# The edges' fields behind the second block's low parts and its first encoder group, and two statistics moved ahead of the edges' copy

## The reference, cut to what matters

```
h  = relu(layernorm(x))                       # x is 1250 x 1024
e  = sigmoid(h @ wenc.T + benc)               # 1250 x 500
h2 = e @ conv_weight                          # 1250 x 500
agg = segment_sum(h2[src] * edge_weight, dst) # 20000 edges, sorted by dst
x  = x + (agg + e @ lin_weight.T) @ wdec.T + bdec
h  = relu(layernorm(x))
x  = x + D^-1/2 (A + I) D^-1/2 (h @ W.T + b)  # A: the same edges
```

## Time and profile before

| | |
|---|---|
| median of 3 runs | 470.28 us (470.02 to 470.74) |
| the profiled execution's own time | 471.0 us |
| its span, first to last instruction | 469.1 us |
| PE busy | 461.9 us, 98% |
| DVE busy | 317.0 us, 68% |
| ACT busy | 208.0 us, 44% |
| granted TensorE clock | 0.999 of full speed (2.4 GHz) |

### The profile page before, as it was taken

One profiled execution on the slowest core, in us unless ns is written; L12 is line 12 of the kernel. 1 busy time (PEld: TensorE's weight loads), 2 busy tenths in 40 slices (PEclk: granted clock), 3 DMA queues, 4 the chain that ended last, 5 costly groups with the idle time before them and its releaser, 6 DMA issues.

```text
span 469.1 us, 9224 instructions
## 1 busy us (share of the span) xinstructions
PE 461.9 (98%) x3452; PEld 401.6 (86%) x3452; DVE 317.0 (68%) x594; ACT 208.0 (44%) x412; POOL 47.0 (10%) x62
## 2 busy tenths in 40 slices
PE   7999999999999999999999999999999999999997
PEld 6999999978888888889888878888889988888886
DVE  6999997777857851594668886928552467567642
ACT  6986797645541141232444444547442522222220
POOL 3722110000000000000000000465500000000000
PEclk9999999999999999999999999999999999999999
DMA  8720848482214570639530005161969415546542
GB/s 306 261 82 23 156 83 219 126 316 77 70 64 85 114 245 0 114 110 342 201 120 1 0 1 213 58 247 68 369 235 381 139 44 226 203 179 224 198 167 99
DMA packets 46111, 72.35 MB, mean 154 GB/s; under 512 B 25292, under 2 KB 34142, under 8 KB 44402
## 3 DMA queue, kind: packets, MB, share of 16 engines
q1 hardware_dynamic: 45746, 71.34, 46.1%
q0 software_dynamic: 320, 0.39, 0.4%
HBM read 44.33 MB, written 22.01 MB: 141 GB/s over the span
## 4 chain that ended last, share of the span: by engine, by line
PE 78%; DVE 9%; DMA 5%; ACT 4%; issue 2%; POOL 2%; POOLq 0%; DVEq 0%; SPq 0%; ACTq 0%
PE bank L1429 18%; PE bank L1445 18%; PE bank L1430 18%; PE bank L1431 18%; DVE weighted L1349 3%; DMA row_scratch<-dis 2%; PE bank L1547 2%; DMA raw<-adj_scratch 2%; DMA dis_row<-row_scratch 1%; PE bank L1549 1%; PE bank L1551 1%; DVE stats L1062 1%; ACT before L874 1%; PE bank L1567 1%; DVE deg L1301 1%
## 5 line engine op out<-in xcount | busy, mean ns | idle before, releaser
L1445 PE MATMUL bank<-a,h_hi 128*128 128x256 f16 (+3 forms) x400 | 85.5, 270 | 0.0
L1445 PE MATMUL bank<-a,h_lo 128*128 128x256 f16 (+3 forms) x400 | 85.5, 270 | 0.0
L1429 PE MATMUL bank<-right,left 128*128 128x512 f32 (+1 forms) x148 | 56.1, 379 | 0.0
L1430 PE MATMUL bank<-right,left 128*128 128x512 f32 (+1 forms) x148 | 55.9, 378 | 0.0
L1431 PE MATMUL bank<-right,left 128*128 128x512 f32 (+1 forms) x148 | 55.9, 378 | 0.0
L1414 DVE SCALAR_TENSOR_TENSOR x<-bank,dis_u,x 128x512 f32<-128x512 f32 (+2 forms) x37 | 26.7, 721 | 36.0 <-PE bank L1431 35.8
L1026 ACT CAST left<-zs 128x512 fp32r<-128x512 f32 x35 | 21.6, 624 | 61.2 <-PE bank L1431 61.1
L1429 PE MATMUL bank<-unit,g 128*128 128x500 f32 (+3 forms) x120 | 42.3, 353 | 0.4 <-DVE unit L1286 0.4
L1445 PEld LDWEIGHTS bank<-a,h_hi 128*128 128x128 f16 (+1 forms) x400 | 39.0, 97 | 4.1 <-issue 0.3
L1445 PEld LDWEIGHTS bank<-a,h_lo 128*128 128x128 f16 (+1 forms) x400 | 39.1, 98 | 3.7
L1431 PE MATMUL bank<-unit,g 128*128 128x500 f32 (+3 forms) x120 | 42.3, 352 | 0.0
(11 more groups left out here) (163 smaller groups left out, 1110.2 us busy)
## 6 DMA issues: line engine op xcount, KB each, us to landing
right_scratch<-right SPq DMA_DIRECT2D x5, 2048.0 KB, 8.2
right<-right_scratch SPq DMA_DIRECT2D x5, 2048.0 KB, 8.0
whole<-w SPq DMA_DIRECT2D x7, 1024.0 KB, 7.5
adj_scratch<-stage SPq DMA_DIRECT2D x50, 125.0 KB, 2.1
raw<-adj_scratch SPq DMA_DIRECT2D x2, 2500.0 KB, 9.8
h<-x SPq DMA_DIRECT2D x9, 512.0 KB, 5.9
x<-x SPq DMA_DIRECT2D x9, 512.0 KB, 6.5
out<-x SPq DMA_DIRECT2D x18, 256.0 KB
```

The lines of the kernel that those rows point to most:

```text
L1429: pe.matmul(o, lhs[0], rhs[0], start=first, stop=False, skip_group_check=True)
L1430: pe.matmul(o, lhs[0], rhs[1], start=False, stop=False, skip_group_check=True)
L1445: ins = pe.matmul(o, h1[i][0:n, k, 128 * f:128 * (f + 1)], moving, start=(k == 0 and part == 0 and i == 0), stop=(k == T - 1 and part == p ...
```

## The change

`POOL_CUTS` goes: the low parts of `we` 3 and 4 are made by DVE with the others, behind the last quarter of block 0, and `EARLY` takes the low parts of `we` in the order 3, 4, 5, 6, 7 at its end. POOL's memsets (`pads`) come before the cuts and wait for POOL's own second block of statistics instead of the cuts. On DVE the three last `lo` steps of block 1's transposes move from behind `fields` to before it. The encoder group (1,0) moves ahead of `edges`; the statistics of tiles 6 and 7 move from behind encoder group (1,1) to between (1,0) and `edges`. The step that was called `half` is renamed `stats0`.

```diff
-POOL_CUTS = (3, 4)
-EARLY += [(0, 0, 4), (0, 1, 4), (0, 0, 5), (0, 1, 5), (0, 0, 6), (0, 1, 6), (0, 1, 7), (0, 0, 7), (1, 0, 5), (1, 0, 3), (1, 0, 6), (1, 0, 4), (1, 0, 7)]
+EARLY += [(0, 0, 4), (0, 1, 4), (0, 0, 5), (0, 1, 5), (0, 0, 6), (0, 1, 6), (1, 0, 3), (0, 0, 7), (0, 1, 7), (1, 0, 4), (1, 0, 5), (1, 0, 6), (1, 0, 7)]
...
-    steps = [("idents",)] + first[:3] + [("half", 2)] + first[3:] + [("starts",), second[0], norms(0)[0], second[1], norms(0)[1], second[2]]
-    steps += cut_we[:3] + t0[:2] + lo(t0[0]) + [t0[2]] + lo(t0[1]) + [t0[3]] + lo(t0[2]) + cut_we[3:5] + lo(t0[3]) + cut_we[5:]
-    steps += [second[3], ("pads",)] + norms(1)
+    steps = [("idents",)] + first[:3] + [("stats0", 2)] + first[3:] + [("starts",), second[0], norms(0)[0], second[1], norms(0)[1], second[2], ("pads",)]
+    steps += cut_we[:3] + t0[:2] + lo(t0[0]) + [t0[2]] + lo(t0[1]) + [t0[3]] + lo(t0[2], t0[3]) + cut_we[3:]
+    steps += [second[3]] + norms(1)
...
-    steps += [third[3]] + lo(e[1]) + [e[2], ("fields",)] + lo(e[2], t1[1], t1[2]) + [e[3]] + lo(t1[3]) + norms(2)[1:]
-    dense = [("edges",)]
+    steps += [third[3]] + lo(e[1], t1[1], t1[2], t1[3]) + [e[2], ("fields",)] + lo(e[2]) + [e[3]] + norms(2)[1:]
+    dense = []
...
-        (1, 0): turn(2), (1, 1): fourth, (1, 2): [("norm", 6)], (1, 3): [("norm", 7), ("split", 6), ("turn", 6)],
+        (1, 0): turn(2), (1, 1): fourth[2:], (1, 2): [("norm", 6)], (1, 3): [("norm", 7), ("split", 6), ("turn", 6)],
...
-            dense += [("e", b, f)] + beside.get((b, f), [])
+            dense += [("e", b, f)] + (fourth[:2] + [("edges",)] if (b, f) == (1, 0) else []) + beside.get((b, f), [])
...
-                elif s[0] == "cut":
-                    if by_pool(*s[1:]):
-                        cut_lo(pool, nc.gpsimd, s)
                 elif s[0] == "pads":
-                    pool.wait_ge(cut_pool, len(POOL_CUTS))
+                    pool.wait_ge(rstd_ready, 2)
```

More of the change, by code:

```diff
@@ L530, in build @@
         cut_ready = {n: sem(f"{n}_ready") for n in ("we", "wc", "wl", "wd")}
-        cut_pool = sem("cut_pool")
         sig_ready = sem("sig_ready")
@@ L584, in read_done @@
                 eng.wait_ge(bank_free, frees[g] + 1)
-        def by_pool(name, k):
-            return name == "we" and k in POOL_CUTS
         def cut_done(eng, name, k):
[L590 to L593, removed]
+            eng.wait_ge(cut_ready[name], k + 1)
         def cut_lo(eng, ops, s):
@@ L598, in cut_lo @@
             ops.tensor_tensor(parts[1][:, s[2], :], raw_w[:, s[2], :], parts[0][:, s[2], :].bitcast(F32),
-                              ALU.subtract).then_inc(cut_pool if by_pool(*s[1:]) else cut_ready[s[1]], 1)
+                              ALU.subtract).then_inc(cut_ready[s[1]], 1)
         def loaded(eng, name, k):
@@ L1086, in _ @@
                     dve.wait_ge(x_in[t], 16)
-                    statistics(t, h0[t % XRING][0:n, :], t, n, (1,) if ("half", t) in STEPS else (0, 1))
-                elif s[0] == "half":
+                    statistics(t, h0[t % XRING][0:n, :], t, n, (1,) if ("stats0", t) in STEPS else (0, 1))
+                elif s[0] == "stats0":
                     t = s[1]
@@ L1115, in _ @@
                 elif s[0] == "cut":
-                    if not by_pool(*s[1:]):
-                        cut_lo(dve, v, s)
+                    cut_lo(dve, v, s)
                 elif s[0] == "fields":
```

## The result

The changed kernel takes **472.66 us** (median of 12 runs, 471.79 to 477.23), the kernel before, beside it, 470.94 (12 runs, 470.02 to 472.09): ratio 1.0039 [1.0022, 1.0055], slower by about 1.7 us. In a second comparison the same kernel gave 1.0026 [1.0010, 1.0042]. The forecast was 470.5, in a range of 469.2 to 471.2. It was worked out from 470.28, the median of three runs; with 470.94 as the base, 0.7 of the 2.2 us between forecast and measurement is the base, and 1.5 is loss that the forecast did not have. The profiled execution took 471.79 for a span of 470.0.

What follows compares the result with a forecast made beforehand. PE, busy 98% of the span, was taken as the bound. Terms 0.43 + 0.92 + 0.10 - 0.9 + 0.5 - 1.3 = -0.25, a loss, gave 470.28 + 0.25 = 470.5 us; range 469.2 to 471.2.

Steps and rivals of the forecast that it cites:

- The cuts: Weight cuts moved from POOL to DVE: the last ends 0.63 earlier, PE's 0.46 stop goes, PE leads by 0.43 us.
- The fields: At the edges' transposes: PE's stops for fields and a low part's bank go, 0.92 us; e(1,0) is 0.10 shorter.
- The bank wait: Near 33 us PE waits 0.9 us at t(2,3) for e(0,3)'s bank, its low part queued behind two statistics; bounds 0 to 1.3.
- (c): Rival: the wait for e(0,3)'s bank does not come, as DVE reaches the statistics early; 0.9 better, 469.6 us; chance 0.08.
- (d): Rival: fields end behind 30.8 and PE still waits, or memsets hold DVE's cuts; 0.5 worse, 471.0 us; chance 0.07.
- The middle: Window 12's stop, in e(3,0) and e(3,1): shrinks from 0.96 to 0.46 us, 0.5 gained (0.2 to 0.9).
- The load: Adjacency's first load, issued later, delays window 25's write; PE stops at window 31 near 103 us, 1.3 us lost (0 to 1.4).
- rival (a): The adjacency load's tail stays hidden, landing within 9 us as the second load did (8.5): 469.2 us; chance 0.22.
- rival (b): Slower: window 26's write stands behind the adjacency's and wl's loads; 0.7 more with a full 1.4 stop, 471.3 us; chance 0.13.
- The end of the windows: Behind 138 us: order the same, leads and lags carried through to the end unchanged; 0 in the sum.

Runs made afterwards that it cites:

- the counted one: Changed kernel with e(1,0) counted again in the planner's total and spent, so windows and load stand where they stood before: 0.9992 to the kernel before, 470.5 us.
- The repeat: The changed kernel, unaltered, measured again beside the kernel before: 1.0026 [1.0010, 1.0042], 472.22 us.
- late kernels: Kernels with the windows where the change puts them: 0 to 17, and the even ones of the others, one group later than before; no single time.
- statistics behind e(1,1) with the windows in place: Changed kernel with the statistics of tiles 6 and 7 back behind e(1,1) and e(1,0) counted in the planner's total: 1.0015, 471.3 us.
- apart with them late: Changed kernel, windows one group late, tile 6's statistics behind e(0,3)'s low part, tile 7's behind e(1,0)'s, adjacency's load behind window 23: 1.0035, 472.76 us.
- the kernel with three things undone: Changed kernel with statistics of tiles 6 and 7 behind e(1,1), raw load behind window 23, window 48 ahead of the last product: 1.0066, 473.48 us.
- The kernel with the load behind 23: Changed kernel with the adjacency's first load issued behind window 23, the second of a pair, instead of behind window 24: 1.0012, 471.4 us.

## Why the prediction was wrong, step by step

- **The cuts, +0.43: right.** DVE's eight cuts took 669 to 678 ns, none stretched beside the memsets, the last one ended at 19.69. The stop of 0.46 shows best in the two profiles that had the full clock from 9 us on and began the joint groups at nearly the same time, the kernel before (14.77) and the counted one (14.92): from there to block 1's transposes 6.16 and 5.75, 0.41 less. Those transposes start 0.52 to 0.78 earlier in nine profiles with the new cuts, 0.13 to 0.26 in three, and later in three with a lower clock at the start (last section). That the profile after shows 0.78 and not 0.43 is luck of its start: PE began the joint groups at 14.01.
- **The fields, +0.92 and +0.10: right.** PE goes from e(1,0) into the edges with no wait, at 30.43.
- **The bank wait, -0.9: right in place and size** (2.58 - 1.66 = 0.92). e(1,1) starts 0.77 to 0.96 earlier in the two profiles, for a forecast of 0.55; the rest is the start, below. Rivals (c) and (d) fell.
- **The middle, +0.5: wrong, the first of two steps that failed.** The stop in e(3,0) did not shrink by 0.5, it grew by 0.13 (3.68 to 3.81). The chain itself was forecast well: in the profile after, DVE's statistics of tile 9, ACT's normalisation and the copy into the stage of window 8 are these rows.

```profile
53.17 1.28 DVE L1050 BATCH_NORM_STATS2 stats<-h 98x6 f32<-98x512 f32 x2
...
59.21 1.24 ACT L873 ACTIVATE x<-h,nbias,rstd 128x1024 f16<-128x1024 f32 x1 [0.55 <-POOL nbias L817]
...
62.48 0.41 ACT L943 COPY stage<-bank 128x250 f32<-128x250 f32 x1
```

So the stage was there at 62.89, within the 62.5 to 63.0 of the prediction. What failed is the gain drawn from it. PE wants the stage earlier too: it has two windows (0.99) less ahead of e(3,0), and its lead. By the prediction's own numbers the statistics were done 1.65 earlier (56.49 to 54.84) and PE's want moved 1.5 earlier (64.02, which is 61.07 + 2.95, to 62.5), so the stop could shrink by 0.1 or so, not 0.5. Measured, ACT's normalisation moved 1.8 earlier (61.00 to 59.21) and PE's want 1.9 (to 62.09, for the lead was 0.96 and not 0.55). Over the kernels, e(3,0) took 3.66 to 3.88 in 13 of the 17, though it began anywhere from 59.1 to 61.2 us. The others are the two that had just lost 3 us in the windows before it (3.17 and 3.03) and two at 4.16 and 4.34 (statistics behind e(1,1) with the windows in place; apart with them late). So the chain of statistics, scale and normalisation mostly moves with PE, and a lead doesn't shorten the stop.
- **The load, -1.3: right in sum in the profile, 1.30, and in part of it by the other mechanism.** The repeat shows 1.05, and the six late kernels with the load in this place 0.73 to 1.30; rival (a), a load of under 9 us, fell. The pair of windows lost 0.75, not 1.4, since the load took 10.1 us and not 11.1. The rest, 0.55, is the mechanism of rival (b), the write of window 26: issued at 95.5, landed 10.7 us later, at 106.2, and PE was held until 106.67. I had priced (b) as added to a full first stop; the two share one delay. The Trainium skill (DMA: Bandwidth & Descriptors, Queues, rings and completion order) has it that a DMA's semaphore write comes only after the earlier writes of the same DMA engine. The rows agree: 10.0, 10.1 and 10.7 for the write right behind the load in three kernels. The experiments show besides that the write's distance behind the load decides whether PE notices.
- **The end of the windows, 0 in the sum: the second step that failed.** "Behind 138 us the order is the same" holds, but just ahead of 138 it isn't: I had carried the windows' shift to window 24 and not to the end of the list, where window 48 falls behind `swl(0,1)` and stands with 49 right before PE's branch. Cost: 0.54 in the profile (13.78 - 12.74 less the window's 0.49), -0.6 in the repeat.
- **The sum.** By the table's columns the profile shows +0.78 + 0.18 - 0.12 - 1.30 - 0.55 = -1.0, where +0.43 + 0.12 + 0.5 - 1.3 + 0 = -0.25 was forecast: 0.62 is the middle, 0.55 the end, and the start was 0.35 better. The timing says -1.8, so 0.8 us of it is not located; in the repeat it says -1.2 and the columns -1.1. The range left 0.7 above the forecast. By the columns the middle and the end used that up, 1.17 together, less the 0.4 that the start gave; neither would have done it alone. The base, 0.7 higher, and what is not located come on top.

## What to carry to other kernels

When a step leaves a planner's count, print the merged order to its very end and compare every place, not only those under study: here one group in a count moved 34 of 50 windows, and it alone was worth 0.3 to 0.5%. Where a chain and the engine that waits for it both move, take the gain from the difference of the two shifts. An engine's wait and the order that causes it can be a fair price for something later; before undoing it, look who receives what the blocking work makes. A small write in the queue of a large load should stand ahead of it or well behind it: 2.4 us behind cost nothing here, 0.4 us behind cost 0.7 to 1.6.

## What the runs showed of the hardware

**A stop, and a lower clock behind it.** After PE had stood for 2.06 us in the kernel with the statistics behind e(1,1), the granted clock was 0.62 over the next encoder group (it fell from 2.4 to 1.2 GHz for part of it), 1.49 us on top; the kernel with three things undone shows the same pair, a wait of 2.0 us and then 0.62. The stops of up to 1.6 us in the other kernels between block 1 and the end of the windows show no such fall behind them. That the stop is the cause is likely by this, and no run tests it by itself.

**The start differs between executions.** From 14 to 17 us the granted clock was 0.50 in one kernel and 1.00 in another with the same instructions there. The kernel with the load behind 23, and then the counted one:

```profile
14.00:17.00 3.00, 3.00 (x16) 2.88 (x15) 3.00 (x6) 3.00 (x8) 2.62 (x8) 0.50 1.06 330
```

```profile
14.00:17.00 3.00, 3.00 (x25) 2.98 (x24) 3.00 (x6) 3.00 (x7) 2.62 (x8) 1.00 1.03 319
```

Sixteen matmuls against 25 in the same time, both with PE busy throughout. Block 1's transposes started at 21.6 instead of 20.2 to 20.8 in the three kernels with the first row's clock. Two more profiles had 0.79 there and started at 20.7 to 20.8. Each kernel has one profile, so whether an edit makes one or the other likelier isn't known; but the kernel before, too, had runs at a lower clock. Of 23 runs of the kernel before in one comparison, four had a granted clock of 0.993 over the whole run, with a median of 471.67 us, and eighteen had 0.996 or 1.000, with medians of 470.55 and 470.51; where in the run the clock was low isn't recorded for them. This may be why ratios of kernels with the same distances differ by 0.1 to 0.2%.

**A branch not taken** (with the value load that it tests) cost PE 0.13 us behind 15 short matmuls of a window (0.62 less 0.49), 0.7 behind 30 of them (1.67 less 0.99), and nothing that shows behind a product's long ones (5.52 for two products, 5.50 to 5.54 in the others). Why 30 hide less than 15 isn't settled.
